# Turning the first pair's maxima ahead of the last masks, and other moved steps, in a graph-network kernel on Trainium2

## The reference, cut to what matters

```python
def gat_conv(x, src, dst, W, a_src, a_dst, bias, H, C, n):       # L0, twice
    h = (x @ W).reshape(n, H, C)
    e = leaky_relu((h * a_src).sum(-1)[src] + (h * a_dst).sum(-1)[dst], 0.2)
    ee = exp(e - segment_max(e, dst)[dst])
    alpha = ee / segment_sum(ee, dst)[dst]
    return segment_sum(alpha[:, :, None] * h[src], dst).reshape(n, H * C) + bias
def rgat_conv(x, W, q, k, b, src, dst, etype, heads, ...):        # L1, twice
    xr = einsum('nd,rdf->rnf', x, W)
    alpha = leaky_relu(xr[etype, dst] @ q + xr[etype, src] @ k, 0.2)
    ...                                                           # the same softmax over dst
x = layernorm(x + (concat(x, gat(gat(layer_norm(x)))) @ Wu + bu))
x = layernorm(x + rgat(elu(rgat(x))))
```

## Time and profile before

| | us |
|---|---|
| time, median of 3 runs (lowest to highest) | 1921.78 (1919.73 to 1922.69) |
| the profiled execution: its time | 1923.26 |
| the profiled execution: its span | 1921.4 |
| PE busy | 1782.4 (93%) |
| DVE busy | 1549.6 (81%) |
| ACT busy | 727.2 (38%) |

### The profile page before, as it was taken

The page is one execution under the profiler, slowest core; times in us unless marked ns, Lnnn a source line. Parts: engine busy times, 40 slices in busy tenths (PEclk is TensorE's granted clock), DMA queues, the critical chain, the costliest instruction groups (busy, mean ns, idle before and its releaser), DMA issues.

```text
span 1921.4 us, 24266 instructions
## 1 busy us (share of the span) xinstructions
PE 1782.4 (93%) x8426; PEld 1338.4 (70%) x8427; DVE 1549.6 (81%) x2949; ACT 727.2 (38%) x1247; POOL 19.1 (1%) x40
## 2 busy tenths in 40 slices
PE   4789978599999899999999999997999989999997
PEld 3534545499854455555899999997999975555554
DVE  7799868999568554999999999996556648998996
ACT  4878966543224221111444444342321222332331
POOL 0000001000000000000000000000000000000000
PEclk8989988799999899999999999998999999999999
DMA  6200149441360326776422212121266467767764
GB/s 183 68 13 27 51 146 394 153 134 56 89 196 17 144 78 212 239 239 198 148 62 67 78 57 86 59 59 33 71 207 215 144 222 261 253 220 247 257 209 167
DMA packets 168068, 276.66 MB, mean 144 GB/s; under 512 B 11819, under 2 KB 132386, under 8 KB 164486
## 3 DMA queue, kind: packets, MB, share of 16 engines
q1 hardware_dynamic: 114342, 211.25, 33.7%
q10 hardware_dynamic: 50336, 49.66, 8.0%
q0 software_dynamic: 3264, 14.16, 2.0%
HBM read 219.31 MB, written 55.71 MB: 143 GB/s over the span
## 4 chain that ended last, share of the span: by engine, by line
PE 47%; DVE 2%; DMA 1%; ACTq 0%; ACT 0%; issue 0%; DVEq 0%; SPq 0%
PE ps L1373 20%; PE ps L1402 17%; PE ps L1233 9%; DMA work<-hs_d 1%; ACTq L1588 0%; PE ps L1181 0%; DMA work<-in_w_d 0%; DVE feat L2124 0%; ACT work L1599 0%; DVE work L2342 0%; ACT counts L1606 0%; DVEq L556 0%; DVE counts L2194 0%; DVE work L2132 0%; DVE work L2135 0%
## 5 line engine op out<-in xcount | busy, mean ns | idle before, releaser
L1402 PE MATMUL ps<-work 128*128 128x384 f32 (+1 forms) x784 | 256.7, 486 | 4.7 <-DVE work L2113 4.7
L1324 PE MATMUL ps<-work 128*128 128x384 f32 (+1 forms) x720 | 238.8, 493 | 4.5 <-ACT work L1699 2.6
L1373 PE MATMUL ps<-counts,work 128*128 128x193 f32 x1440 | 239.3, 327 | 0.1
L1373 PEld LDWEIGHTS ps<-counts,work 128*128 128x128 f32 x1440 | 235.9, 190 | 0.4 <-DVE work L2348 0.4
L1793 ACT ACTIVATE work<-work,s 128x1280 f32<-128x1280 f32 x112 | 152.6, 1363 | 209.9 <-DVE work L2342 209.9
L1402 PEld LDWEIGHTS ps<-work 128*128 128x128 f32 x784 | 148.7, 190 | 109.9 <-DVE work L2113 5.9
L1324 PEld LDWEIGHTS ps<-work 128*128 128x128 f32 x720 | 137.4, 191 | 102.5 <-issue 17.0
L2348 DVE SCALAR_TENSOR_TENSOR work<-work,counts 128x1280 f32<-128x1280 f32 x112 | 166.6, 1488 | 1.4 <-ACT work L1793 1.3
L1373 PE MATMUL ps<-counts 128*128 128x193 f32 x960 | 160.9, 327 | 1.4 <-POOLq L556 1.4
L1373 PEld LDWEIGHTS ps<-counts 128*128 128x128 f32 x960 | 157.4, 190 | 2.0 <-POOLq L556 2.0
L1954 DVE TENSOR_SCALAR work<-work,winoff 125x480 bf16<-125x480 f16 x480 | 158.3, 404 | 0.4 <-issue 0.3
(11 more groups left out here) (292 smaller groups left out, 2597.0 us busy)
## 6 DMA issues: line engine op xcount, KB each, us to landing
work<-hs_d SPq DMA_DIRECT2D x75, 960.0 KB, 5.4
work<-nomask_d SPq DMA_DIRECT2D x70, 320.0 KB, 3.2
work<-pqrow_d SPq DMA_DIRECT2D x12, 1280.0 KB, 6.2
nomask_d<-work SPq DMA_DIRECT2D x40, 320.0 KB, 7.0
hx_d<-work ACTq DMA_DIRECT2D x60, 192.0 KB, 2.5
counts<-hx_d SPq DMA_DIRECT2D x120, 96.0 KB, 1.9
hs_d<-feat ACTq DMA_DIRECT2D x22, 480.0 KB, 3.6
counts<-pqrow_d SPq DMA_DIRECT2D x6, 1280.0 KB, 6.4
```

What stands on the lines that cost most here:

```text
L1324: last = mm(bank(n % 4 if i else n % 2, cols), xT[:, j, t * P:(t + 1) * P], wv[:, j, :], start=(j == 0), stop=(j == DT - 1))
L1373: last = mm(sums_at(c, t, u), xe_of(c)[i % RING][:, t * P:(t + 1) * P], hx[:, i % RING, 0:1 + c.width], start=(r == 0 and k == 0 and t % T ...
L1402: last = mm(bank(product_bank(g, i), width), a[:, at * P:(at + 1) * P], h_block(n, block_, width), start=(m == 0), stop=(m == STEPS_D - 1) ...
```

## The change

- The 20 projection groups lie at windows 24 to 75 and not 24 to 79. The reciprocal of `deviations` stands after window 22 and not 19; the twelve steps of `centre` lie two and two after windows 19 to 24.
- On the last tile of the masks DVE does `rows_of_maxima(0)` before the last three masks; PE turns the pair and ACT copies it before these masks; SP stores and loads the pair's rows before the last three mask stores. The last tile's searches of heads 2 and 3 move into attention A, behind steps 2 and 4.
- Before barrier 0 DVE makes the exponents of steps 0 and 1, ACT loads its exp table and does exp 0, SP loads the first five feature tiles. To make room `nm_out` and `nm_total` change places.
- In A `rows_of_maxima(1)` comes at step 5, and the second pair is turned, copied and stored at 6, 8 and 11.
- In C exp 0 stands one group earlier on ACT (`EXP_GROUP_C` 57).
- Barrier 4 is gone. SP issues D's first weights once the last step of C is used; the last save of C runs over the tiles 0, 5, 2, 3, 4, 6, 7, 8, 9, 1, with the two first `low` behind tile 5 and the two first `up` behind tile 4.
- In D the rows of the second type are loaded behind step 4's block (was 1), those of the third behind step 8's (was 4).

```diff
-M_WINDOWS, G_WINDOWS, STATS_WINDOWS = (1, 18), (22, 80), (4, 18)
-SQRT_AFTER, CENTRE_AFTER = 18, (20, 22)
+M_WINDOWS, G_WINDOWS, STATS_WINDOWS = (1, 18), (22, 76), (4, 18)
+SQRT_AFTER, RECIPROCAL_AFTER, CENTRE_FROM, CENTRES = 18, 22, 19, 2
-PAIR_TURN_AT, PAIR_COPY_AT, PAIR_OUT_AT = 2, 4, 7
-PQ_GROUP_C, PQ_MASK_C, EXP_GROUP_C = 42, 46, 58
+PAIR_AT = {"a": (5, 6, 8, 11), "c": (1, 2, 4, 7)}
+SEARCHES_LATE = [(2, 2), (4, 3)]
+PQ_GROUP_C, PQ_MASK_C, EXP_GROUP_C = 42, 46, 57
+LAST_BEFORE_UP = 4
+LAST_SAVE_ORDER = [0, 5, 2, 3, 4, 6, 7, 8, 9, 1]
...
             for n, (r, t) in enumerate(MASKS):
+                if n == 4 * T - RELS:
+                    sp.wait_ge(pq_c, 1)
+                    sp.dma_start(pqrow_d[0:4, :], pair_rows[0][0:4, :]).then_inc(pq_out, 16)
+                    sp.wait_ge(pq_out, 16)
+                    sp.wait_ge(v_done, 11)
+                    sp.dma_start(pqb_a[0], pqrow_d[0:2, :].partition_broadcast(P)).then_inc(s.pq_in[0].sem, 16)
                 sp.wait_ge(nm_copied, n + 1)
...
             for i in range(MASKS_OUT):
                 sp.wait_ge(*nm_out_s[i].at(16 * ring_share(RELS * T, i, MASKS_OUT)))
+            for i in range(3):
+                sp.wait_ge(*s.hx_out[i].at(16 * ring_share(2 * T, i, 3)))
+            for k in range(RING):
+                sp.dma_start(hx_a[:, k, 1:1 + HA], ga_d[k * P:(k + 1) * P, 0:HA]).then_inc(s.hx_in[k].sem, 16)
             for landed in total_out:
...
+                sp.wait_ge(*sems[C].p_used.at(RING + C.heads * C.R * T))
+                w_load_d(sp, s, 0)
...
-                            if g == 0 and m == 1:
+                            if g == 0 and m == H_SLOTS:
                                 pq_rows_d(ci, s, 1)
-                            if g == 0 and m == H_SLOTS:
+                            if g == 0 and m == 2 * H_SLOTS:
...
-            end_phase(sp, 4)
             layer(3, DD, 5)
...
             for n in range(4 * T):
+                if n == 4 * T - RELS:
+                    pe.wait_ge(pq_ready, 1)
+                    turn_pair(A, 0, PAIR_0_PS)
                 pe.wait_ge(nm_ready, n + 1)
...
+                pe.wait_ge(*sems[C].saved.at(6 * T))
                 for q, name in ORDER_D:
...
+            nc.scalar.activation(mm_[0:1, 0, 0:1], epsc[0:1, :], ACT.Exp)
+            act.wait_ge(*s.x_ready.at(STEP_CREDIT + 1))
+            nc.scalar.activation(xe_a[0], xe_a[0], ACT.Exp, bias=s02[:, 0, 0:1], scale=0.8).then_inc(s.exp_done.sem, 1)
             end_phase(act, 0)
...
                     if t == T - 1:
                         rows_of_maxima(0)
+                        for n in masks:
+                            no_edges(n)
...
+                if c is A:
+                    dve.wait_ge(v_turned, len(WT_HALVES))
+                    for i in range(2):
+                        exponents(i, i, i, 0, 0, 16, 0, NP)
+                    for i in range(MASKS_OUT):
+                        dve.wait_ge(*nm_out_s[i].at(16 * ring_share(RELS * T, i, MASKS_OUT)))
+                    v.memset(hx_a[:, :, 0:1], 1.0).then_inc(ones, 1)
...
+                            for step, h in SEARCHES_LATE if c is A else []:
+                                if i == step:
+                                    search_a(T - 1, h)
```

199 lines of the change are left out of this document (104 added, 95 removed).

## The result

| | before | after |
|---|---|---|
| median, us (runs) | 1920.76 (4) | 1907.54 (4: 1905.15 to 1909.12) |
| ratio of the times | | 0.9932, 95% interval 0.992 to 0.9945 |
| profiled execution: time, span | 1923.26, 1921.4 | 1906.95, 1905.1 |

The change gains 13.2 us by the medians; 19.6 had been forecast. The time lies within the range (1896.5 to 1909.5), 5.3 us above the forecast of 1902.2.

A forecast was written before the change was run, and what follows sets the result against it. PE bounds the kernel, busy 93% of the span. Terms 5.1 + 1.0 + 9.4 + 1.0 - 1.4 + 0.2 + 1.9 + 2.4 = 19.6 us, off the 1921.78 median, give 1902.2; range 1896.5 to 1909.5.

The forecast's parts named there:

- the rivals: Weight loads limit again (1906.2, or 1905.1 by a GpSimd rule), chance 0.17; attention A no earlier (1905.8 or 1908), 0.13.
- The square root's wait: Windows: DVE's 5.64 us wait goes, first group starts at 106.0, last ends at 255.6; gain 5.1 us.
- The first mask: End of the windows: PE's first turning no longer waits for ACT's copy of the last group; gain 1.0 us.
- The first weight load: First score rows: PE's 8.15 us wait goes, full clock gives 1.3 more; together 9.4 us (6 to 10.5).
- The mask stage: Before attention A: DVE makes the three last masks after the maxima, so the pair is ready 1.2 us earlier.
- weight loads become the limit again: Rival, chance 0.17: mask stage at the DMA engines' pace and a late first load cost 4 us, giving 1906.2.
- the rule beside it: First weight load: GpSimd descriptors wait while DVE holds shared ports; load lands at 270.4, 2.9 late, giving 1905.1.
- Attention A's start: Before attention A: SP enters the barrier last at 368.1, PE starts at 369.8, not 370.86; gain 1.0 us (-1 to 2.5).
- the 369 named as a sign of being wrong: In front of attention A: SP entering barrier 0 after 369 in the frame of before would show the forecast wrong.
- the rival's 371: Rival, chance 0.13: the pair's load lands with the stores at 366, so attention A starts at 371; 1905.8.
- The searches in attention A: Attention A: 2.8 us more DVE work before the first save, PE stalls in step 10; cost 1.4 us (0 to 3).
- Borders and D's first steps: C's start gains 0.2 us, D's border 1.9; PE's 2.36 us wait in D's third step goes, gain 2.4.

The follow-up runs named there:

- a_swap: Changed kernel with PE's two branches around the windows exchanged, the never-taken path standing first; 1906.62 us, ratio 0.9921.
- a_mask0: Changed kernel with the last tile's total moved behind the first two searches, so DVE can make the first mask earlier; 1904.2 us, ratio 0.992.
- a_g80: Changed kernel with the 20 projection groups back over windows 22 to 79; 1906.26 us, ratio 0.9926.
- a_hx1: Changed kernel with one feature load of attention A ahead of the barrier and four behind it, instead of five ahead; 1906.07 us, ratio 0.9923.
- c_short: Changed kernel with one feature load before the barrier, late searches back, last tile's total after two searches, never-taken path without groups and units; 1901.58 us, ratio 0.99.
- a_nolate: Changed kernel with the last tile's two searches back ahead of attention A; 1905.26 us, ratio 0.9911.
- a_rows1: Changed kernel with the second edge type's rows of D loaded ahead of the third block again; 1910.71 us, ratio 0.9941.

## Why the prediction was right, and where it fell short

The direction, most of the terms and the range held; the forecast's own band of 1900 to 1904.5 did not. The measured 1907.54 lies where the rivals had put it (1905.1 to 1908), yet neither of the loads that they name was what held it: that the number fits them is luck.

**The square root's wait (right, larger than forecast).** The wait went whole, and the first group stood at 104.3 against 106.0. Window 24, which I had charged at 2.56, took 1.38 (103.10). From there to the last group's end it took 150.4 us, forecast 149.6, and ACT's last copy ran from 261.66 to 262.23, forecast 261.5. This arithmetic held to 1 us.

**The first mask (the step that failed).** "PE's first turning 4.02 after it ... another 1.0": I let the first mask follow the last copy by 3.0 us, because that was the distance before less a wait. It came at 266.96 and not at 264.6. Before, the last group's 4.14 us of PE work stood over the jump, and nothing in the trace showed it; the change takes that group away. That is the case of a cover that goes: I asked what hides the weight load, and did not ask what the moved group itself hid. Of the 2.4 us lost, 1.1 lie in front of the jump (DVE's masks start at 265.04, `265.04 1.29 DVE L2055`, and in a_swap, with no jump there, PE follows such a start by 0.63 us, which gives 265.67) and the other 1.3 are the jump's; a_mask0 shows the jump's whole length.

**The first weight load (right in mechanism, a little less).** The 8.15 us went whole. But "PE also stays at the full clock" failed: after 5.34 us of idling the first three masks and the score rows took 1.9 us longer than at full clock. M0 to SR1 gained 8.45 and not 9.4. a_g80 shows besides that these terms were split wrongly: 6.1 for the windows and 9.4 for the load. With the groups left in place (a_g80) the windows' part alone moves the second score rows by 8.9 us, and the load's part adds only 3.2, because the load's wait is paid for by the jump and the clock.

**The mask stage.** Forecast 1.2 (three masks behind the maxima), found 0.35 in this profile and up to 3.8 in a_hx1's. What goes with the spread is the clock behind the DVE waits (2.10, 2.04 and 2.82 us), not the DMA engines: a_hx1 passes the same bytes in 61.3 us, with a share of 1.03 from 284 to 304 as in the changed kernel. The rival "weight loads become the limit again" did not happen; in the changed kernel no score rows waited for a load. Nor did the rule beside it (descriptors of a GpSimd DMA blocked beside a fast DVE; the Trainium skill, "SBUF — State Buffer", section "SBUF: two separate sides") come out in time: c_short's load is issued at 255.13 beside one-hots that go on to about 261, and its score rows start at 265.38, where the rule as I had applied it gave 270.4; whether the one-hots run in such a fast mode no run here shows. The trace of c_short (same columns as above) has the DMA engines full while DVE still works:

```profile
255.10:258.00 2.90, 2.15 (x11) 0.84 (x9) 2.90 (x9) 2.51 (x7) 2.74 (x3) 1.00 0.34 41
258.00:261.50 3.50, 2.55 (x12) 1.03 (x12) 2.18 (x8) 1.94 (x4) 0.00 (x0) 1.00 1.01 377
```

**Attention A's start (the order right, 1.3 us short).** SP was the last into the barrier, as forecast, behind five issues (2.22 us for 2.0). The stores that it waits for landed later: its feature loads start 9.3 us behind the pair's load, where my bound gave 8.35. In the frame of before that puts SP into the barrier at 369.2 and PE's first step at 371.1. The one is past the 369 named as a sign of being wrong, the other is the rival's 371, but not by its cause: the pair's load took 6.6 us to land for 5.8 and did not come with the stores. In the span the start came 11.0 us earlier and not 16.5; the loss at the first mask and in the mask stage makes up the rest. a_hx1 shows that only SP's issues hold this barrier. "Two searches leave, so DVE is ready at 361.7: the load is what is late now" was the right sentence, and I did not draw its consequence: an engine that ends up waiting anyway does not gain by work taken from it. a_nolate puts it at 0.1 us.

**The searches in attention A (right).** A stall in step 10 of 1.23 us (1.4 forecast), 1.9 us for the whole of A; the rest of the 1.9 was not followed.

**Borders and D's first steps (right).** C's barrier gave 0.3 (0.2 forecast). At D's border DVE turns the weights (`1320.90 1.54 DVE L2196`) 7.9 us behind the last product instead of 10.3, and PE's first product gains 1.6 (1.9 forecast). D's steps gained 2.1 (2.4 forecast), and a_rows1 takes 2.2 back. PE still waits 2.00 us in the second step and now 0.56 in the fifth.

In sum: 2.4 at the first mask, 0.95 at its clock, 0.85 in the mask stage, 1.3 in front of A, 0.5 in A, 0.5 in D, together 6.5 us.

## What to carry to other kernels

Before work is moved away from a place, ask what it covered there, also on its own engine's sequencer: behind PE's branch with a long untaken side, 4.14 us of queued work hid the jump. Putting the untaken side ahead of the taken one moves the jump to the start, where 1.3 to 2.6 us of its 4.2 were still there at the first group. A releaser that ends just before its waiter goes on may be no more than the last of several; when the waiter starts 1.5 us after its named releaser, move the releaser and look again. Take the gains of moved work only where the engine that loses it was the last one: a load that lands later makes it worth nothing, as the two searches were.

## What the runs showed of the hardware

- A jump of PE over at least 480 instructions cost 5.4 us of idling (a_mask0) and 4.2 us at the start of the program (a_swap), one over a short piece at most 0.9 (c_short). The profile calls this idling "issue", or names another engine that happened to be late too. A 16 KB packet of kind "instruction" goes with the long jump, at either place.
- After the same wait of 2.10 us PE's clock fell in one profile (matmuls at 2.78 us for twelve) and not in another (1.49). The mask stage of some 22 MB took 61.3 to 65.7 us in kernels that differ little in it, layer B 418.0 to 424.9. These spreads are of the size by which executions of one kernel differ (1899.94 to 1910.73 for a_hx1). That they are the cause of it is not shown, since each kernel has one profile.
